# mLSTM gate products in a two-block transformer kernel: tokens stationary, 32 weight columns moving, turned back by transposes

## The reference, cut to what matters

```
h_in  = rmsnorm(x)                                   # [4, 256, 256]
i_pre = cap(h_in @ w_ig + b_ig)                      # w_ig: [256, 8 heads]
f_pre = cap(h_in @ w_fg + b_fg)                      # cap(a) = 15 tanh(a / 15)
Fcum  = cumsum(log_sigmoid(f_pre), over tokens)
Dmat  = Fcum[s] - Fcum[t] + i_pre[t], causal
m     = max over t of Dmat ;  Smat = exp(Dmat - m)   # weights of the heads
```

## Time and profile before

| | |
|---|---|
| median of 3 runs | 673.02 us (672.11 to 673.04) |
| the profiled execution's own time | 672.34 us |
| its span, first to last instruction | 670.6 us |
| PE busy | 658.1 us (98% of the span) |
| DVE, ACT, POOL busy | 438.3, 411.3, 246.7 us |

### The profile page before, as it was taken

The page is one execution under the profiler, slowest core; times in us unless marked ns, Lnnn a source line. Parts: engine busy times, 40 slices in busy tenths (PEclk is TensorE's granted clock), DMA queues, the critical chain, the costliest instruction groups (busy, mean ns, idle before and its releaser), DMA issues. The chain is left out here.

```text
span 670.6 us, 15275 instructions
## 1 busy us (share of the span) xinstructions
PE 658.1 (98%) x5297; PEld 633.0 (94%) x5297; DVE 438.3 (65%) x968; ACT 411.3 (61%) x1085; POOL 246.7 (37%) x279
## 2 busy tenths in 40 slices
PE   8999999999999999999999999999999999999995
PEld 8999999999999999999999899999987799999995
DVE  6556557557666655765665576556569986556877
ACT  5556677666776666866577773334689864333553
POOL 3731972134353133632328555112451462222011
PEclk9999999999999999999999999999999899999999
DMA  7174654435534436534363404000166100000000
GB/s 254 37 219 160 193 172 140 133 101 174 168 127 113 127 108 185 161 128 126 97 183 124 111 1 151 32 0 2 48 208 243 65 1 1 1 1 0 1 33 31
DMA packets 38172, 69.74 MB, mean 104 GB/s; under 512 B 3440, under 2 KB 22640, under 8 KB 37872
## 3 DMA queue, kind: packets, MB, share of 16 engines
q1 hardware_dynamic: 37696, 68.38, 32.8%
q10 hardware_dynamic: 432, 0.79, 0.4%
HBM read 52.18 MB, written 16.97 MB: 103 GB/s over the span
## 5 line engine op out<-in xcount | busy, mean ns | idle before, releaser
L312 PE MATMUL PJ<-xTh,WBh 128*128 128x256 f32 x364 | 106.7, 293 | 0.3 <-POOL WBl L839 0.3
L314 PE MATMUL PJ<-xTh,WBl 128*128 128x256 f32 x364 | 103.0, 283 | 0.0
L313 PE MATMUL PJ<-xTl,WBh 128*128 128x256 f32 x364 | 102.8, 283 | 0.0
L824 POOL TENSOR_TENSOR stage<-stage 128x256 f32<-128x256 f32 x32 | 24.5, 766 | 165.0 <-DVE stage L691 165.0
L584 ACT ACTIVATE probs<-probs,rinv 128x256 f32<-128x256 f32 x128 | 58.4, 507 | 26.7 <-DVE rinv L707 26.7
L1202 PE MATMUL UG<-xTh,WBh 128*128 (+1 forms) x256 | 73.6, 288 | 0.3 <-PEq L54 0.3
L1205 PE MATMUL UG<-xTh,WBl 128*128 (+1 forms) x256 | 72.4, 283 | 0.0
L1203 PE MATMUL UG<-xTl,WBh 128*128 (+1 forms) x256 | 72.4, 283 | 0.0
L1274 ACT ACTIVATE ga<-UG 128x256 f32<-128x256 f32 x64 | 24.5, 383 | 75.1 <-PE UG L1205 75.1
L312 PEld LDWEIGHTS PJ<-xTh,WBh 128*128 128x128 f32 x364 | 69.6, 191 | 0.9 <-issue 0.5
L313 PEld LDWEIGHTS PJ<-xTl,WBh 128*128 128x128 f32 x364 | 69.6, 191 | 0.0
(11 more groups left out here) (320 smaller groups left out, 2385.9 us busy)
## 6 DMA issues: line engine op xcount, KB each, us to landing
K<-scr_k SPq DMA_DIRECT2D x60, 256.0 KB, 4.3
raw<-in_w_att SPq DMA_DIRECT2D x37, 256.0 KB, 4.7
Q<-scr_q SPq DMA_DIRECT2D x15, 512.0 KB, 7.5
stage<-scr_m SPq DMA_DIRECT2D x6, 768.0 KB, 5.9
scr_q<-rot_h SPq DMA_DIRECT2D x30, 128.0 KB
scr_q<-rot_l SPq DMA_DIRECT2D x30, 128.0 KB
scr_k<-rot_h SPq DMA_DIRECT2D x30, 128.0 KB
scr_k<-rot_l SPq DMA_DIRECT2D x30, 128.0 KB
```

The lines of the kernel that those rows point to most:

```text
L312: pe.matmul(out, ah, bh, start=(i == 0), stop=False)
L313: pe.matmul(out, ah, bl, start=False, stop=False)
L314: last = pe.matmul(out, al, bh, start=False, stop=(i == n - 1))
L824: pool.tensor_tensor(y[:, 0:S], c[:, 0:S], sn[:, S:2 * S], ALU.subtract).then_inc(rope_sum, 1)
```

## The change

The roles of the operands of the gate products are swapped. A tile of 128 tokens (high or low part) becomes stationary, and 32 columns of gate weights move over it: 8 input-gate and 8 forget-gate columns, each as high and low part (`GATES` = 16, two times). The padded weight block shrinks to these columns, so ACT's rounding and DVE's subtraction of the gate weights work on 32 elements a partition where they had 896. A batch takes 2 token tiles x 4 products = 8 products, which leave [128 tokens, 32] in `OUTS`. (Low token parts are multiplied with the low weight columns too, a term that was left out before.)

Then DVE adds high-weight and low-weight results with two reductions of 128 elements a partition (`add_gates`) into `gate_tok`, a part of `gt` that a new memset of 128x512 has cleared at the start of the layers, and PE turns the result with four 128x128 transposes (`gates_T`) into the two sums that the tanh reads, which now both lie in `X`.

The order is rewritten too. On PE the gate products of batches 0 to 2 stand between the halves of project(0), those of batch 3 between the q/k and the v/o halves of batch 1, and `gates_T` behind the first v/o half of batch 1. On ACT `gates()` is split in two (tanh and exp; ln), with one output-gate tanh of batch 1 between them, and the pieces of `mlp_hi` are placed differently. On DVE the splits of batch 0 move ahead of, and between, the norm of batch 3, and `add_gates` stands between the two splits of batch 1.

```diff
+GATES = 2 * HM
...
-        gate_w = WI[:, :, :].rearrange("p a n -> p (a n)")[:, 12 * PIECE - 4 * KT * WIDE:]
-        WGh, WGl = (gate_w[:, i * 2 * KT * WIDE:(i + 1) * 2 * KT * WIDE].rearrange("p (t g n) -> p t g n", t=KT, g=2)
-                    for i in range(2))
+        WG = WI[:, 11, PIECE - KT * 2 * GATES:].rearrange("p (t l n) -> p t l n", t=KT, l=2)
+        WG_part = [WG[:, :, l, :].rearrange("p t (g h) -> p t g h", g=2) for l in range(2)]
...
-        gate_sums = (X[:, 0:S], OUTS[:, 1, 0:S])
+        gate_parts = OUTS[:, 1, 0:B * TT * 2 * GATES]
+        gate_tok = gt[:, :, :].rearrange("p a s -> p (a s)").rearrange("p (t g k) -> p t g k", t=TT, g=2)
+        gate_sums = (X[:, 0:S], X[:, S:2 * S])
...
-                w = slice(96 - 32 * c, 96 - 32 * c + P)
-                for n, out in enumerate(gate_sums):
-                    for i in range(3 * KT):
-                        t, (a, b) = i // 3, ((WGh, xh_v), (WGh, xl_v), (WGl, xh_v))[i % 3]
-                        last = pe.matmul(out, a[:, t, n, w], b[:, t, c, :], start=(c == 0 and i == 0),
-                                         stop=(c == B - 1 and i == 3 * KT - 1))
+                for t in range(TT):
+                    rows, at = slice(t * P, (t + 1) * P), (TT * c + t) * 2 * GATES
+                    for i in range(2 * KT):
+                        last = pe.matmul(gate_parts[:, at:at + 2 * GATES], (xh_v, xl_v)[i % 2][:, i // 2, c, rows],
+                                         WG[:, i // 2, :, :], start=(i == 0), stop=(i == 2 * KT - 1))
+                if c == B - 1:
+                    last.then_inc(s_["gates_ready"], 1)
+
+            def gates_T():
+
+                pe.wait_ge(s_["gates_added"], 2)
+                for n in range(2):
+                    for t in range(TT):
+                        last = pe.transpose(gate_sums[n][:, t * P:(t + 1) * P], gate_tok[:, t, n, :], ident[:, :])
                 last.then_inc(s_["gates_ready"], 1)
...
-            project(0)
-            for c in range(B - 2):
-                project_gates(c)
+            project_part(0, 0)
+            project_gates(0)
+            project_part(0, 1)
+            project_gates(1)
+            project_vog(0, 0)
+            project_gates(2)
+            project_vog(0, 1)
             pe_T(pe, 1, B - 1)
-            project_gates(B - 2)
-            project_qk(1)
+            project_part(1, 0)
+            project_part(1, 1)
             project_gates(B - 1)
-            project_vog(1)
+            project_vog(1, 0)
+            gates_T()
+            project_vog(1, 1)
             project(2)
             rows_T()
             project(3)
...
-            mlp_hi(0, 5)
+            mlp_hi(0, 2)
+            evac_q(0)
+            mlp_hi(2, 3)
+            evac_k(0)
             act_ssq(act, 1, 3)
-            evac_q(0)
-            evac_k(0)
+            mlp_hi(3, 5)
+            act_hi(act, 1, 3)
             evac_og(0)
-            act_hi(act, 1, 3)
-            mlp_hi(5, 6)
             evac_q(1)
-            mlp_hi(6, 7)
             evac_k(1)
+            mlp_hi(5, 7)
+            gates_tanh()
+            evac_og(1, range(1))
+            gates_log()
+            evac_og(1, range(1, TT))
+            evac_q(2)
             mlp_hi(7, 8)
-            gates()
-            evac_og(1)
-            mlp_hi(8, 9)
-            evac_q(2)
-            mlp_hi(9, 10)
             evac_k(2)
-            mlp_hi(10, 12)
+            mlp_hi(8, 10)
             evac_og(2)
+            mlp_hi(10, 11)
             exp_nm()
+            mlp_hi(11, 12)
             evac_q(3)
             evac_k(3)
...
+            dve.memset(gt[:, :, :], 0.0).then_inc(s_["consts_set"], 1)
             dve_stats(dve, 0, B - 2)
             ffn_dve(dve, 0)
...
+            def add_gates():
+
+                dve.wait_ge(s_["gates_ready"], 1)
+                dve.wait_ge(s_["consts_set"], 4)
+                parts = gate_parts.rearrange("p (c t l g h) -> p g c t h l", c=B, t=TT, l=2, g=2)
+                for n in range(2):
+                    out = gate_tok[:, :, n, :].rearrange("p t (c k) -> p c t k", c=B)[:, :, :, 0:HM]
+                    dve.tensor_reduce(out, parts[:, n], axis=AX.X, op=ALU.add).then_inc(s_["gates_added"], 1)
...
             add_out(dve, 0, 3)
             dve_stats(dve, 1, 3)
+            split_q(0)
             dve_apply(dve, 1, 3)
+            split_k(0)
             dve_xs(dve, 1, 3)
-            split(0)
+            take_v(0, 0)
+            take_v(0, 1)
             dve_lo(dve, 1, 3)
-            split(1)
+            split_q(1)
+            add_gates()
+            split_k(1)
+            take_v(1, 0)
+            take_v(1, 1)
             chain()
             split(2)
```

More of the change, by code:

```diff
@@ L1001, in layers @@
         stage1 = sb("stage1", [P, HM * 384])
-        wg_f = stage1[:, 0:2 * KT * WIDE].rearrange("p (t g n) -> p t g n", t=KT, g=2)
+        wg_f = stage1[:, 0:2 * KT * WIDE].rearrange("p (t g n) -> p t g n", t=KT, g=2)[:, :, :, 96:96 + HM]
         A = [a[:, :].rearrange("p (h n) -> p h n", h=HM) for a in (stage, stage1)]
@@ L1017, in layers @@
             xt_ready xt_hi xt_split x_added scaled stored
-            bgs_ready qk_ready qk_hi qk_split vog_ready v_taken og_ready gates_ready gates_tanh sp_ready
+            bgs_ready qk_ready qk_hi qk_split vog_ready v_taken og_ready gates_ready gates_added gates_tanh sp_ready
             chain_step m_ready nm_ready m_out masked_rows rows_ready gcol_ready enm_ready
@@ L1476, in project_gates, with project_part @@
+                if c == B - 1:
[5 more added lines that the diff above has]
+                        last = pe.transpose(gate_sums[n][:, t * P:(t + 1) * P], gate_tok[:, t, n, :], ident[:, :])
                 last.then_inc(s_["gates_ready"], 1)
-            def project_qk(c):
+            def project_part(c, i):
                 if c == 0:
@@ L1481, in project_qk @@
                     pe.wait_ge(s_["wl_split"], LP - 1)
[L1482 to L1497, removed]
+                else:
+                    pe.wait_ge(s_["qk_split"], 2 * c - 1 + i)
@@ new lines, in project_part, with project_vog @@
+                for n in range(2):
+                    w = slice((2 * i + n) * P, (2 * i + n + 1) * P)
+                    last = six(UG[i][:, n * S:(n + 1) * S], [(WLh[:, t, w], WLl[:, t, w]) for t in range(KT)],
+                               x_parts(c))
+                last.then_inc(s_["qk_ready"], 1)
+            def project_vog(c, t):
+                if c:
+                    pe.wait_ge(s_["og_ready"], 2 * (c - 1) + t + 1)
+                rows = slice(t * P, (t + 1) * P)
+                six(UG[2 + t][:, :], [(xh_v[:, f, c, rows], xl_v[:, f, c, rows]) for f in range(KT)],
+                    [(WLh[:, 2 + f, :], WLl[:, 2 + f, :]) for f in range(KT)]).then_inc(s_["vog_ready"], 1)
@@ L1499, in project @@
             def project(c):
-                project_qk(c)
-                project_vog(c)
+                project_part(c, 0)
+                project_part(c, 1)
+                project_vog(c, 0)
+                project_vog(c, 1)
             def rows_T():
@@ L1647, in _ @@
             act.wait_ge(s_["wg_in"], 16)
-            act.activation(WGh, wg_f, ACT.Copy).then_inc(s_["wg_hi"], 1)
+            act.activation(WG_part[0], wg_f, ACT.Copy).then_inc(s_["wg_hi"], 1)
             act.wait_ge(s_["small_in"], 16 * 4)
@@ L1661, in evac_k, with evac_og, gates_tanh @@
                                scale=cols[:, C_SIGN:C_SIGN + 1]).then_inc(s_["qk_hi"], 1)
-            def evac_og(c):
-                for t in range(TT):
+            def evac_og(c, which=range(TT)):
+                for t in which:
                     act.wait_ge(s_["v_taken"], 2 * c + t + 1)
                     act.activation(og_v[:, c, t, :], UG[2 + t][:, D:2 * D], ACT.Tanh, scale=0.5).then_inc(s_["og_ready"], 1)
-            def gates():
-                act.wait_ge(s_["gates_ready"], B)
+            def gates_tanh():
+                act.wait_ge(s_["gates_ready"], 2)
                 act.wait_ge(s_["bgs_ready"], 1)
@@ L1678, in gates, with gates_log @@
                 act.activation(gt[:, 1, :], gt[:, 1, :], ACT.Exp, scale=-CAP).then_inc(s_["gates_tanh"], 1)
+            def gates_log():
                 act.wait_ge(s_["gates_tanh"], 2)
@@ L1823, in _ @@
             dve.wait_ge(s_["wg_hi"], 1)
-            dve.tensor_tensor(WGl, wg_f, WGh.bitcast(F32), ALU.subtract).then_inc(s_["wg_split"], 1)
+            dve.tensor_tensor(WG_part[1], wg_f, WG_part[0].bitcast(F32), ALU.subtract).then_inc(s_["wg_split"], 1)
             dve.wait_ge(s_["small_in"], 64)
             dve.tensor_scalar(bgs[:, :], bg[:, :], 1.0 / CAP, None, ALU.mult).then_inc(s_["bgs_ready"], 1)
+            def add_gates():
+                dve.wait_ge(s_["gates_ready"], 1)
+                dve.wait_ge(s_["consts_set"], 4)
+                parts = gate_parts.rearrange("p (c t l g h) -> p g c t h l", c=B, t=TT, l=2, g=2)
+                for n in range(2):
```

(2 more changed lines are left out.)

## The result

The median of the kernel after is 681.13 us over four executions (671.92, 680.85, 681.41, 686.19); before it was 672.57 beside them. The ratio is 1.0076, with an interval of 1.0038 to 1.0113. (All ratios here leave out executions more than 1.5% above the fastest of their kernel, so I give the times themselves as well.) Forecast were 671.6 and a range up to 673.4; the kernel became slower instead of faster. The four times are spread over 14 us, where before's lie within 1. The profile is of the execution of 671.92; two causes must be told apart, one that is in it and one that is not.

The account below looks back on a forecast made before the run. The order of PE's work was taken to bound the projections; PE saves 1.5 us (-5.7 + 3.76 + 0.44), capped by the read-back to -1.4, so 673.02 - 1.4 = 671.6 us, range 670.3 to 673.4.

Parts of the forecast that it names:

- The PE terms: Projections on PE: -5.7 for old gate products, +3.76 for 32 narrow ones, +0.44 for `gates_T`, in sum -1.5 us.
- Rival A: Gate blocks on PE: short products run without overlap, up to 0.19 us each, giving 674.3; chance 0.07.
- The chains: ACT and DVE up to the heads: `M` ready 0.1 later, `evac_q(3)` at 498.3, first `weigh` 1.35 to 1.5 us sooner.
- Rival C: Projections to heads: ACT and DVE keep most of the gain, first `weigh` only 0.5 to 0.9 sooner, 672.3; chance 0.17.
- I cost the read-back at +0.1: Read-back of `M` ahead of the heads: it comes only 0.1 us later, as the gate chain gets no shorter.
- the covers of 0.8 and 1.6 us: Masks waiting for the read-back of `M`: slack used up to a tenth, so the gain cannot be much over 1.5.
- rival D: Heads: the clock fall at 520.9 disappears because they start elsewhere, about 1 us more gain, 670.6; chance 0.06.
- the mask of batch 1: DVE in the heads: its first mask moves from 506.70 to 505.25, behind its transfer landing at 505.1.
- Behind that, the heads and the MLP follow relative to their start: Everything behind the first `weigh`: unchanged but shifted with the start, except transfers that hang on `M`.
- Rival B: Gate blocks at 476 to 490: the clock falls for 3.4 us, costing about 1.4; 673.0, or 673.7 with late `M`; chance 0.10.

Follow-up runs that it names:

- e9: Kernel after plus 12 short 32-column warming products at the very start, to move the instruction packet: ratio 1.0015, three of 12 above 677, profiled execution 670.61.
- e10: Kernel before with 10 wide warming products of 512 columns instead of 22 of 256: median 674.43 against 673.07, ratio 1.0009, none of 12 above 677.
- e1: Kernel after run again, unchanged: 674.41 to 686.78 us, five of six above 677, ratio 1.01.
- e14: Kernel after, unchanged, on the chip and in the rounds of later runs: six of six above 677, profiled execution 686.51.
- e7: Kernel after plus 24 no-operations in PE's list ahead of the projections, which left no trace: median 682.74, eight of 12 above 677.
- e3: Kernel after with PE's old order, the narrow gate products in contiguous blocks: ratio 1.0031, four of 10 above 677.
- e2: Kernel after plus an unread 512-column product ahead of each four gate products: ratio 1.0031, one of 10 above 677.
- e4: Kernel after's new order with the old wide gate products: ratio 1.0023, two of 10 above 677.
- e11: Kernel after plus 12 short warming products and one unread product ahead of the first scores: ratio 0.9996, two of 12 above 677.
- e13: Kernel after with seven instead of four unread products behind the first scores, nothing else changed; no time of its own is given.
- e16: Kernel after plus 12 short warming products and seven instead of four unread products behind the first scores: none of 12 above 677.
- e12: Kernel after plus 12 short warming products and seven instead of four unread products behind the first scores; expected median 671.5 and ratio 0.998 not reached.

## Why the prediction was wrong

**The PE terms held.** The narrow products cost 0.11 each, the lower bound, not the 0.1175 of the scores; `gates_T` cost 0.45 for 0.44. The Trainium skill (TensorE: Matmul & The Clock Gate, section LDWEIGHTS) gives 107 ns for a load of 128 columns; this trace has 111 ns a product (0.89 for eight), 4 more. Rival A is out. PE saves 5.7 - 4 x 0.89 - 0.45 = 1.7 us, where 1.5 was forecast. Because the span's first microseconds differ from one execution to the next, I read the rest against the write of `M`, 0.44 later in the profile after (494.03 against 493.59).

**The chains held.** `evac_q(3)` came at 498.44, with no wait for PE, 498.0 by `M`'s clock (forecast 498.3). `M` was written 19.75 us after the first product of the projections (494.03 - 474.28), where it had been 19.8 (493.59 - 473.8); I had +0.1. Rival C is out: e9's `weigh`, without the late read-back, came 1.11 sooner by the trace's clock and 1.25 by `M`'s, against a forecast of 1.35 to 1.5.

**First failed step: "I cost the read-back at +0.1".** The read-back was issued 2.05 later (497.68 against the earlier trace rows), 1.6 of it by the second write and 0.44 by the later `M`. I had looked at what must be ready before it and at how long its own transfers take, and had seen that the covers of 0.8 and 1.6 us were used up. I had taken the two writes of `M` as a constant. They are not: 12 products fewer in PE's list had moved an instruction packet onto them. The term costs 1.3 us of waiting on DVE, which is 0.84 at the first `weigh` (beside e9, by `M`'s clock), and takes most of the gain there away; the undisturbed execution stands at 671.92 for 672.34. What is left of a gain in it is 0.4 at the first `weigh` by `M`'s clock, and the fall at 520.9, which is gone (rival D, worth some 0.6: the span is 0.6 shorter with a start 0.44 later). That the packet's place decides over the write, e9 and e10 show in both directions; that it is the packet, and not something else that the shifted list brings, rests on its place in all 18 profiles, ten slow and eight fast. For the mask of batch 1 I had forecast 505.25; it came at 506.73.

**Second failed step: "Behind that, the heads and the MLP follow relative to their start".** This is the 9 us. Rival B had the right kind, a falling clock, but put it into the gate blocks and priced it by the one fall of the trace, 3.4 us long, at 1.4. (Its own 673.7 with a late `M` should have been the upper end of the range, where 673.4 stands.) The gate blocks kept the full clock in every profile. The fall comes in the heads, 1.7 to 5 us behind the first scores in the four profiles that have it, and lasts 24 us in e1 (679.43) and 38 us in e14 (686.51). It makes PE, which had 0.7 of spare time there in 16 us, the bound. The earlier trace rows had shown how near the edge the heads run, and I used them only for the size.

How easily it comes is shown by runs that change only this: three wide products fewer behind the first scores bring long executions into the kernel before (8 of 12, where before has 0 of 143); three more take nearly all of them out of the kernel after (2 of 24, where after has 22 of 28, e7 counted with it). So the kernel before stood just on the safe side, held there by four products that nobody reads. (Three products more or fewer also shift the packets behind them by as much; no run separates the two.) How the change moved it over is in part argued: its first scores come behind a wait of PE instead of directly behind products of 512 columns. The counts of the kernels with four unread products behind the scores and none ahead of them fit, though they come from several chips: with that wait in the profile (after, e3) 26 of 38 are above 677, with the read-back in time and no wait (e2, e4, e9) 6 of 32; and e10, late read-back but no wait, has none of 12. But the wait isn't all of it: e9 falls in 3 of 12 without it, and the undisturbed execution of the kernel after and the disturbed one of e1 are alike up to the fall, wait included. What decides between two executions of one kernel, and what in the change besides the wait makes the start of the heads more sensitive, stays open.

The Trainium skill (same page, section HAM oscillation — how this bites in real kernels) puts the loss of the clock down to idle gaps of PE between bursts. The traces agree in part: all four profiles with the long fall have a wait of PE ahead of the first scores (0.71 in e1, 1.38 in e7, 0.40 in e11, 1.05 in e14). But e13 has 1.46 and no fall, and in the row at half clock in e1 PE is busy in 8.00 of 8.00 us by the profile, and the clock does not come back.

**Is the change worth having?** That is not shown. With the packet moved and seven unread products, the fastest times are 670.43 and 670.77, beside 671.73 and 671.72 of the kernel before on the same chips, 1.3 and 1.0 less, near the 1.4 that was forecast for the median. The medians, 672.10 and 672.31 against 673.20 and 672.85, have ratios whose intervals include 1. This is the best version found, and no more than equal by this measurement. What spreads every kernel's times between about 671 and 675 lies in large part at the start: in e13 the clock was at 0.59 between 8 and 12 us, and `M` was written 1.5 us later than in the profile after (495.50 for 494.03). The 12 short products may cost something there: in e16's profile (and e11's) they take 2.58 us instead of e12's 1.47, PE issues 20 products between 8 and 12 us where e12 issues 36, and `M` is written at 497.42 instead of 494.37. Two of the four profiles with them are like this, none of the others; more than that no run shows.

## What to carry to other kernels

When an edit takes instructions out of an engine's list, the packets that bring its later instructions land elsewhere: look up which small, critical transfer they meet, and if one has no cover, move them with cheap instructions early in the program, and look at what these cost where they stand. When an engine is sped up to the point where it waits, ask what clock the sparse stretch behind the wait will get, and price a fall by that stretch's whole length and not by the one fall seen. Take ten or more times, beside the kernel before on the same chip: a kernel that stands at such an edge gives 671.9 or 686.2 with the same code, and one profile shows only one of them.

## What the runs showed of the hardware

- One 16 KB instruction packet near a 64 KB write went with a rise of its time from issue to landing from 1.6 to 3.3 us (after; 3.2 in e10, 2.9 to 3.8 in all ten profiles that have it), and moving it away brought 1.6 back (e9).
- Products of only 32 columns, each with a new load of 128 columns, followed each other every 0.11 us (after).
- The granted clock stayed at half for 24 us (e1), 27 us (e11) and 38 us (e7, e14) with PE busy throughout; it came back at 531 in e1, with no change in PE's order of work that I could name.
- No-operations in PE's list left no instruction in the trace and did not move a packet (e7: it began 0.9 behind the first write of `M`, as in e1).
